# Two-layer cross-attention on one core: a chain of eight VectorE operations spread over the maxima steps, and a Gram tile with four matmuls fewer

## What is computed

```
layer 0:  text = first 77 tokens, ip = the other 298
          out = softmax(q k_text) v_text + softmax(q k_ip) v_ip
          x1  = x + out @ Wo + bo
layer 1:  text = first 371 tokens, ip = the last 4
          probs_t  = softmax(q k_text)
          qsem     = l2norm(probs_t @ text)
          sem      = qsem . l2norm(ip)                 (4 numbers per row and head)
          probs_ip = softmax(q k_ip + 0.5 * sem) * spatial_mask
          out = probs_t v_text + probs_ip v_ip
          y   = x1 + out @ W_out + b_out
```

## Time and profile before

| | us |
|---|---|
| median of 3 runs | 2545.01 |
| lowest to highest | 2544.80 to 2546.96 |
| the profiled execution | 2546.61 |
| its span in the trace | 2544.8 |
| TensorE busy | 2462.8 (97%) |
| TensorE weight load busy | 2130.8 (84%) |
| VectorE busy | 1636.7 (64%) |
| ScalarE busy | 1226.3 (48%) |
| GpSimd busy | 766.4 (30%) |

### The profile page before, as it was taken

One profiled execution on the slowest core, in us unless ns is written; L12 is line 12 of the kernel. 1 busy time (PEld: TensorE's weight loads), 2 busy tenths in 40 slices (PEclk: granted clock), 3 DMA queues, 4 the chain that ended last, 5 costly groups with the idle time before them and its releaser, 6 DMA issues.

```text
span 2544.8 us, 64183 instructions
## 1 busy us (share of the span) xinstructions
PE 2462.8 (97%) x26500; PEld 2130.8 (84%) x26500; DVE 1636.7 (64%) x3217; ACT 1226.3 (48%) x2251; POOL 766.4 (30%) x998
## 2 busy tenths in 40 slices
PE   7899999999999999999999999999999999999998
PEld 7788888888888888888888888888888888888877
DVE  4465667766667666667656677666677556676665
ACT  3355444455444455444554444554444554444543
POOL 3133233233233232233332323332332332332322
PEclk9999999999999999999999999999999999999999
DMA  9775446674456754456655466745566645566611
GB/s 215 138 107 86 88 84 99 107 117 74 86 86 96 117 89 86 89 90 112 103 87 89 85 101 103 107 75 89 97 95 108 91 81 88 90 95 105 94 26 21
DMA packets 371689, 241.45 MB, mean 95 GB/s; under 512 B 131947, under 2 KB 365243, under 8 KB 371388
## 3 DMA queue, kind: packets, MB, share of 16 engines
q1 hardware_dynamic: 371398, 237.35, 57.1%
HBM read 171.35 MB, written 64.59 MB: 93 GB/s over the span
## 4 chain that ended last, share of the span: by engine, by line
PE 77%; DVE 13%; POOL 4%; DMA 2%; issue 2%; ACT 1%; SPq 1%; DVEq 0%; POOLq 0%; ACTq 0%
PE ST L820 7%; PE R L886 6%; PE R L762 5%; PE PN L859 5%; PE R L775 4%; PE R L776 4%; PE R L707 4%; DVE m L1068 4%; PE R L708 4%; POOL w L1444 3%; PE R L944 3%; PE R L778 3%; PE PN L904 3%; PE R L710 3%; PE R L889 3%; PE R L891 3%
## 5 line engine op out<-in xcount | busy, mean ns | idle before, releaser
L1444 POOL TENSOR_TENSOR w<-w 128x448 f32<-128x448 f32 (+1 forms) x256 | 328.8, 1284 | 378.8 <-DVE w L977 360.6
L980 DVE SCALAR_TENSOR_TENSOR w<-p,pr 128x1344 f32<-128x1344 f32 x160 | 296.0, 1850 | 166.7 <-ACT pr L1330 151.0
L1302 ACT ACTIVATE p<-ST 128x1344 f32<-128x1344 f32 x260 | 335.4, 1290 | 101.8 <-PE ST L823 97.4
L886 PE MATMUL R<-pr,Gh 128*128 128x448 f32 (+1 forms) x960 | 366.2, 381 | 0.8 <-issue 0.8
L977 DVE TENSOR_TENSOR rem<-R,kst 128x298 f32<-128x298 f32 (+2 forms) x180 | 89.4, 497 | 428.3 <-ACT kst L1185 428.3
L977 DVE TENSOR_TENSOR w<-R,w 128x448 f32<-128x448 f32 (+1 forms) x480 | 281.5, 619 | 68.8 <-PE R L891 57.8
L1378 POOL TENSOR_TENSOR kst<-rem,kst 128x298 bf16<-128x298 f32 (+2 forms) x180 | 147.9, 822 | 534.5 <-ACT kst L1185 293.2
L775 PE MATMUL R<-wvh,ch 128*128 128x320 f32 (+3 forms) x896 | 303.4, 339 | 1.1 <-DVE rem L977 1.1
L776 PE MATMUL R<-wvh,cl 128*128 128x320 f32 (+3 forms) x896 | 277.9, 310 | 0.0
L820 PE MATMUL ST<-Qs,Ks 100*128 100x112 bf16 (+1 forms) x3520 | 229.3, 214 | 10.3 <-ACT p L1302 3.5
L820 PEld LDWEIGHTS ST<-Qs,Ks 100*128 100x128 bf16 (+1 forms) x3520 | 188.1, 98 | 48.6 <-issue 13.9
(11 more groups left out here) (221 smaller groups left out, 5930.9 us busy)
## 6 DMA issues: line engine op xcount, KB each, us to landing
Ks<-k_split SPq DMA_DIRECT2D x384, 140.6 KB, 5.7
Ks<-k_split SPq DMA_DIRECT2D x384, 93.8 KB, 8.0
w<-in_ctxT SPq DMA_DIRECT2D x31, 750.0 KB, 9.5
k_split<-kst SPq DMA_DIRECT2D x64, 281.2 KB
k_split<-kst SPq DMA_DIRECT2D x64, 223.5 KB, 2.9
Qs<-q_split SPq DMA_DIRECT2D x64, 210.0 KB, 8.6
q_split<-qst SPq DMA_DIRECT2D x128, 84.0 KB, 2.4
Qs<-q_split SPq DMA_DIRECT2D x64, 140.0 KB, 8.7
```

What stands on the lines that cost most here:

```text
L886: e.matmul(r[0:nj, 0:QW], Gh[0:ROWS[u], q:q + nj], x[0:ROWS[u], QW * u:QW * u + QW], start=u == 0, stop=False)
L980: return e.scalar_tensor_tensor(out=to, in0=x, scalar=s, in1=y, op0=op0, op1=op1)
L1302: e.activation(to.rearrange("p (u q) -> p u q", u=3), st, ACT.Exp).then_inc(p_whole, 1)
L1444: e.tensor_tensor(first, first, w2[n % 2][0:ROWS[j], QW * j:QW * j + QW], ALU.add).then_inc(ns_added, 1)
```

## The change

It has three parts.

1. `fuse` and `ip_softmax` become eight stages of one VectorE operation each (`root_inverse`, `sem`, `fuse`, `fuse_max`, `fuse_less`, `ip_sum`, `ip_inverse`, `ip_softmax`). From a maxima step to the next one of them is taken. `ip_T`, `ip_mm`, `o_T` and `o_mm` come later in the list by it.
2. The pieces get other counts, in all rounds but the first and the last two.
3. The third Gram tile takes 8 matmuls in place of 12. GpSimd copies the four ip columns of the low context `cl` behind the high context `ch` (`c_image`), so the products of high with high and of high with the low ip columns come in one matmul of 124 columns; the product of low with high is made once (120 columns), and VectorE adds it and its transposed use in three further operations. `w4` waits for these.

```diff
@@ finish1
-        o.add("fuse", b)
-        yield
-        o.add("ip_softmax", b)
-        yield
+        for step in ("root_inverse", "sem", "fuse", "fuse_max", "fuse_less", "ip_sum", "ip_inverse", "ip_softmax"):
+            o.add(step, b)
+            yield
@@ between
-            if count[0] in (1, 2, 3, 5, 7, 9, 10):
+            if b + 1 == B:
+                take(last, (0, 1, 5, 3, 0, 1, 0, 1, 0, 1, 1)[count[0]])
+            elif count[0] != 13:
                 take(last, 1)
-            if count[0] in (2, 4, 6, 8, 11, 12, 14, 16):
+            if count[0] in ((2, 3, 5, 6, 8, 11, 13, 15) if 0 < b < B - 1 else (2, 4, 6, 8, 11, 12, 14, 16)):
                 take(pieces, 1)
@@ tensor, "g"
+                    if t == 2:
+                        w.wait_ge(c_image, b + 1)
+                        for k in range(4):
+                            e.matmul(r[0:n, first:T + 1 + NIP], h[:, k, first:first + n], h[:, k, first:T + 1 + NIP],
+                                     start=k == 0, stop=k == 3)
+                        for k in range(3):
+                            e.matmul(r[0:n, 0:T + 1 - first], lo[:, k, first:first + n], h[:, k, first:T + 1], start=k == 0,
+                                     stop=False)
+                        e.matmul(r[0:n, 0:T + 1 - first], lo[:, 3, first:first + n], h[:, 3, first:T + 1], start=False,
+                                 stop=True).then_inc(g_mm, 1)
+                        continue
@@ vector, "g"
+                    if t == 2:
+                        lo.then_inc(dve_step, own.one())
+                        r, made = R[slot["R", ("g", b, t)]], own.n
+                        tt(g4[0:n, 2, :], r[0:n, T + 1:T + 1 + NIP], g4[0:n, 2, :], ALU.add).then_inc(dve_step, own.one())
+                        w.wait_ge(dve_step, made)
+                        lo_ = Gl[0:n, q:q + n]
+                        tt(lo_, r[0:n, 0:n], lo_.bitcast(fp32), ALU.add)
+                        w.wait_ge(dve_step, own.n)
+                        tt(g4[0:n, 2, :], r[0:n, n:n + NIP], g4[0:n, 2, :], ALU.add).then_inc(g_lo, 1)
+                        continue
@@ vector (the other seven stages are cut in the same manner)
+                elif kind == "root_inverse":
+                    w.wait_ge(d_root, b + 1)
+                    e.reciprocal(sm[0][:], d2[:]).then_inc(root_inverted, 1)
...
@@ scalar
-                elif kind == "fuse":
+                elif kind == "fuse_less":
@@ gpsimd
-                    w.wait_ge(g_hi, at("g", b, 2))
+                    w.wait_ge(g_lo, at("g", b, 2))
...
+                    w.wait_ge(c_low, 4 * (b + 1))
+                    e.tensor_copy(ch[b % 2][:, :, T + 1:T + 1 + NIP], cl[b % 2][:, :, T - NIP:T]).then_inc(c_image, 1)
```

More of the change, by code:

```diff
@@ L434, in stage_order @@
         take(rows0, 9)
-        for n in (17, 0, 0, 2, 5, 3, 0):
+        for n in (17, 0, 0, 0, 0, 0, 0, 0, 0, 2, 5, 3, 0):
             take(last, 1)
@@ L484, in xattn_two_layers @@
         tx = sb("tx", [128, 4, NT])
-        ch = [sb(f"ch{i}", [128, 4, T + 1], f32r) for i in range(2)]
+        ch = [sb(f"ch{i}", [128, 4, T + 1 + NIP], f32r) for i in range(2)]
         cl = [sb(f"cl{i}", [128, 4, T + 1], f32r) for i in range(2)]
@@ L566, in xattn_two_layers @@
         v_mm, v_copied = (sem(n) for n in ("v_mm", "v_copied"))
-        c_hi, c_low, wk_hi, wk_low, c_pads = (sem(n) for n in ("c_hi", "c_low", "wk_hi", "wk_low", "c_pads"))
+        c_hi, c_low, c_image, wk_hi, wk_low, c_pads = (
+            sem(n) for n in ("c_hi", "c_low", "c_image", "wk_hi", "wk_low", "c_pads"))
         g_mm, g_hi, g_lo, g4_scaled, w4_copied = (sem(n) for n in ("g_mm", "g_hi", "g_lo", "g4_scaled", "w4_copied"))
@@ L577, in xattn_two_layers @@
                              "ip_mm", "ip_added", "num_read"))
+        root_inverted, ip_max, ip_summed, ip_inverted = (
+            sem(n) for n in ("root_inverted", "ip_max", "ip_summed", "ip_inverted"))
         o_T, o_T_copied, o_mm, x_added, x1_T, x1_T_copied = (
@@ L1149, in vector @@
                         ALU.max).then_inc(d_bound, 1)
+                elif kind == "root_inverse":
+                    b, = key
+                    w.wait_ge(d_root, b + 1)
+                    e.reciprocal(sm[0][:], d2[:]).then_inc(root_inverted, 1)
+                elif kind == "sem":
+                    b, = key
+                    f1 = fus[1]
+                    w.wait_ge(root_inverted, b + 1)
+                    tt(f1[:], num[:], sm[0][:].unsqueeze(2).to_broadcast([S, H, NIP]), ALU.mult).then_inc(num_read, 1)
                 elif kind == "fuse":
@@ L1152, in vector @@
                     f0, f1 = fus
[L1153 to L1156, removed]
                     w.wait_ge(num_read, b + 1)
                     tt(f0[:], f1[:], sip[b % 2][:], ALU.add).then_inc(fused, 1)
+                elif kind == "fuse_max":
+                    b, = key
                     w.wait_ge(fused, b + 1)
-                    e.reduce_max(sm[1][:], f0[:], X).then_inc(dve_step, own.one())
-                    w.wait_ge(dve_step, own.n)
-                    tt(f1[:], f0[:], sm[1][:].unsqueeze(2).to_broadcast([S, H, NIP]), ALU.subtract).then_inc(fus_less, 1)
+                    e.reduce_max(sm[1][:], fus[0][:], X).then_inc(ip_max, 1)
+                elif kind == "fuse_less":
+                    b, = key
+                    f0, f1 = fus
+                    w.wait_ge(ip_max, b + 1)
+                    tt(f1[:], f0[:], sm[1][:].unsqueeze(2).to_broadcast([S, H, NIP]), ALU.subtract).then_inc(fus_less, 1)
+                elif kind == "ip_sum":
+                    b, = key
+                    w.wait_ge(ip_exp, b + 1)
+                    e.reduce_sum(sm[1][:], fus[0][:], X).then_inc(ip_summed, 1)
+                elif kind == "ip_inverse":
+                    b, = key
+                    w.wait_ge(ip_summed, b + 1)
+                    e.reciprocal(sm[2][:], sm[1][:]).then_inc(ip_inverted, 1)
                 elif kind == "ip_softmax":
@@ L1165, in vector @@
                     f0, f1 = fus
[L1166 to L1170, removed]
+                    w.wait_ge(ip_inverted, b + 1)
                     if b:
```

## The result

| | before | changed |
|---|---|---|
| median, us | 2545.86 (4 runs) | 2636.72 (4 runs) |
| lowest to highest | 2544.80 to 2546.96 | 2624.62 to 2640.68 |
| profiled execution, its span | 2546.61, 2544.8 | 2640.68, 2638.9 |
| granted clock over the span | 0.995 | 0.962 |

The ratio is 1.0349, 95% interval 1.0315 to 1.0383: the change makes the kernel slower by 3.5%. The forecast was 1.3%. The four executions of the changed kernel differ by 16 us, and they stand in the order of their granted clocks: 0.973 with 2624.62, 0.967 with 2636.47 and 2636.98, 0.962 with 2640.68.

The account below looks back on a forecast made before the run. TensorE's path was taken to bound the kernel. Waits of 3.4 us a round, less 2.0 before and 0.4 for the tile, gave 1.07 unrounded, 32 us in thirty rounds: 2577 us, range 2544 to 2595.

Parts of the forecast that it names:

- `ip_T`: TensorE waits ahead of this transpose for VectorE's product, made at 1427.46: 1.35 us lost a round.
- VectorE's two new waits: VectorE waits for ScalarE's copies ahead of the low halves of the first and second Gram tiles: 1.1 and 0.8 us.
- Step 9: TensorE waits ahead of this wide maxima step until VectorE has read step 7: 0.45 us lost a round.
- the last transpose: TensorE waits ahead of the transpose of layer 1's maxima, at the end of the maxima steps: 0.67 us a round.
- Step 10: TensorE waits ahead of this narrow maxima step until VectorE has read step 8: 0.5 us lost a round.
- The maxima steps: The sixteen steps of a round were to take about 26.5 us for 25.45 before.
- the third tile: The third Gram tile's matmuls on TensorE were to take 0.9 us and not 1.3.
- Lost after the change: 0.45 + 0.5 + 1.35 + 0.45 + 0.67 = 3.4 us a round: Sum of TensorE's waits in the changed maxima steps, the second 0.45 being three small waits; before the change 2.0.
- The eight matmuls: Third Gram tile with four matmuls fewer: 0.4 us less a round on TensorE, VectorE's three more operations hidden by idle time.
- VectorE does not fall behind: First rival: VectorE's two waits for Gram copies are not there; 2540 to 2545 us, about the same; chance 0.12.
- `ip_T` finds its weights ready: Second rival: VectorE leads TensorE through steps 8 to 10, so the 1.35 wait goes, or half: 2500 or 2520; chance 0.10.
- the third rival: The chain's links cost the same when spread, so VectorE gains nothing: some 0.4 us more a round, 2589 us; chance 0.10.

Follow-up runs that it names:

- a_fill: Changed kernel with five unread matmuls added on TensorE ahead of its wait for the weights of `ip_T`: 2572.21 us, ratio 1.0113.
- experiment 5: Kernel before with only the third Gram tile changed, to eight matmuls: 2537.93 us, ratio 0.9984.
- experiment 4: Changed kernel with the third Gram tile back in twelve matmuls, the rest kept: 2655.29 us, ratio 1.0453.
- lead2: Changed kernel with the eight chain operations, Gram tiles, `o_T` and `o_mm` at other places, scaled columns and context split later: 2484.10 us, ratio 0.9764.

## Why the prediction was wrong

**Right.** The sign, the places of the waits, and nearly their sizes. `ip_T` was put at 1427.46, 15.71 us into the round; it came 15.64 into it. VectorE's two new waits: forecast 1.1 and 0.8, measured 1.12 and 0.72. Step 9 0.45, measured 0.44; the last transpose 0.67, measured 0.60. Step 10 was 0.5, measured 0.31, and `ip_T` 1.35, measured 1.15 as idle time of TensorE; by the spacing of starts, which the prediction used for the kernel before, these are 0.47 (2203.38 to 2204.01, less 0.16 for a matmul) and 1.31 (2204.37 to 2205.78, less 0.10 for the transpose). The maxima steps were to take 26.5 us and took 26.73 in the round without a fall; the third tile 0.9, from 2206.80 to the next step at 2207.81 it took 1.0. With the clock up the total holds: 32 us forecast, 29 (24 to 33) in a_fill. Part of that is luck. The round that the forecast was read from takes 25.44 us up to the last transpose, while the rounds before without a fall take 25.62 on average. Against the first a round without a fall costs 1.3 us, against the average 1.1, where 1.07 was forecast; the tile (below) brought less than its 0.4.

**The step that failed** is "Lost after the change: 0.45 + 0.5 + 1.35 + 0.45 + 0.67 = 3.4 us a round". It prices each wait at its own length and takes the durations behind the waits from rows at full clock. In 27 of 29 rounds these waits were followed by 3.41 or 6.83 us at 1.2 GHz; by the count above that is 70 us in the profiled execution, by a_fill 64.5 between medians and 60 by the ratios. No rival and no bound of the range had such a term, so the range ended at 2595.

It could have been read ahead. The mean clock before was 0.995 and not 1, and two falls stand in the middle rounds of that trace. One of them, in TensorE's timeline and then by stretch:

```profile
262.57 0.50 PE L802 MATMUL ST<-Ks,Qs 96*112 96x375 bf16 x2 [0.67 <-DVE m L1068]
...
264.19 0.37 PE L802 MATMUL PN<-Ks,Qs 96*112 96x375 bf16 x1 [0.56 <-DVE m L1068]
```

```profile
255.90:264.89 8.99, 7.53 (x48) 6.09 (x45) 8.45 (x27) 4.53 (x10) 0.79 (x1) 1.00 1.10 199
264.89:268.30 3.41, 3.41 (x14) 3.16 (x14) 1.97 (x4) 0.45 (x1) 0.00 (x0) 0.50 0.31 107
```

Two waits, 0.67 and 0.56, close to each other; then 3.41 us at 0.50; and the maxima steps of that round took 25.4 us for 23.4. Ahead of the other fall the waits are 0.69 and 0.56; in six more rounds, with 0.41 to 0.60 in place of the first, the clock stayed up. I forecast 0.45, 0.5 and 1.35 within 3.3 us and did not ask what follows.

**The eight matmuls** were costed at -0.4 a round, with VectorE's idle time as cover, "up to 0.4" if the cover were gone. This term was mis-sized too: they bring 0.02 a round alone (experiment 5) and 0.05 in the changed kernel with the clock up (experiment 4), since TensorE then waits for VectorE further on; in lead2 they bring 0.24.

**The rivals.** "VectorE does not fall behind" and "`ip_T` finds its weights ready" are ruled out by the waits of 1.12 and 1.15. For the third, the spread operation at 2197.66 is 0.23 long and the next starts 0.15 behind its start, so the overlap that the forecast counted on is there. The Trainium skill, "VectorE: DVE Perf Modes", section "The DRAIN you can't avoid", says that the next operation does not start until the pipe is empty, but adds that one which is not held starts earlier. The trace agrees with the addition, which the third rival left out.

**Open.** What decides in the single round. The two rounds shown first have the same waits, and the clock fell in one. The runs bound it: three waits as in the changed kernel, 27 of 29; the long one alone 10; a longer one (1.49) with 0.12 right ahead of it 12, each fall 3.41 long; 0.6 us of the long one left, none.

## What to carry to other kernels

A wait of TensorE can cost more than its length: before pricing one, look in the trace for stretches at half clock, at what TensorE did ahead of them and how much longer the round became. Whether the clock is the cause is told by one cheap experiment, matmuls that nobody reads in the place of the wait, and these are also a remedy (2636.7 to 2574.1 us with two of them). The better remedy is an order without the wait, and then every engine behind it has to be read anew, since what was free in the old order (a copy behind GpSimd, a load behind a store) was next in line.

## What was not expected of the hardware

The granted clock fell to half for 6.83 us behind waits of 0.45, 0.30 and 1.15 us, though TensorE had been busy 14.91 of the 16.83 us up to there. At 0.50 it issued 29 matmuls in 6.83 us, in the same stretch of a round at 1.00 it issued 44. Filling 0.5 us of the longest wait was enough to keep the clock up in all 29 rounds.
